# Finished states of a gated graph network turned by VectorE and a DMA trip in place of TensorE transposes

## What is computed

```python
h = relu(layernorm(x))
q, k, v = h @ Wq.T, h @ Wk.T, h @ Wv.T
rel = adj.T * (q @ k.T);  rel = rel / norm(rel, axis=2)
x = x + rel @ v                                   # attention part
h = relu(layernorm(x))
for _ in range(3):                                # gated part
    a  = adj @ h;  av = concat(a, a)
    z  = sigmoid(av @ w3.T + h @ u3.T + biases)
    r  = sigmoid(av @ w4.T + h @ u3.T + biases)
    c  = tanh(av @ w5.T + (r * h) @ u5.T + biases)
    h  = (1 - z) * h + z * c
x = x + h
```

## Time and profile before

| | us |
|---|---|
| median of 3 runs | 982.24 (981.36 to 982.58) |
| the profiled execution | 981.1 |
| its span, first to last instruction | 978.8 |
| TensorE busy | 960.0 (98%) |
| VectorE busy | 678.8 (69%) |
| ScalarE busy | 501.1 (51%) |
| GpSimd busy | 119.8 (12%) |

### The profile page before, as it was taken

The page is one execution under the profiler, slowest core; times in us unless marked ns, Lnnn a source line. Parts: engine busy times, 40 slices in busy tenths (PEclk is TensorE's granted clock), DMA queues, the critical chain, the costliest instruction groups (busy, mean ns, idle before and its releaser), DMA issues.

```text
span 978.8 us, 15089 instructions
## 1 busy us (share of the span) xinstructions
PE 960.0 (98%) x5256; PEld 829.2 (85%) x5256; DVE 678.8 (69%) x1338; ACT 501.1 (51%) x877; POOL 119.8 (12%) x161
## 2 busy tenths in 40 slices
PE   7799999999999999999999999999999999999996
PEld 7788888888888888888888888888888888888885
DVE  4866768776677776877767767776768766676644
ACT  4455554645446463554725645356544555445542
POOL 1210112102030010200102001110111101020000
PEclk9899999999999999999999999999999999999998
DMA  5011111211022020310203102031010311010001
GB/s 168 1 44 44 39 48 41 90 43 64 21 71 87 13 86 0 128 43 0 86 17 111 43 0 86 21 107 43 25 60 21 107 43 57 28 58 28 1 2 43
DMA packets 41537, 49.43 MB, mean 51 GB/s; under 512 B 4400, under 2 KB 37936, under 8 KB 41520
## 3 DMA queue, kind: packets, MB, share of 16 engines
q1 hardware_dynamic: 41520, 49.20, 15.3%
HBM read 26.12 MB, written 23.07 MB: 50 GB/s over the span
## 4 chain that ended last, share of the span: by engine, by line
PE 96%; DVE 1%; ACT 1%; issue 0%; POOL 0%; DVEq 0%; POOLq 0%
PE gate L357 14%; PE gate L359 13%; PE gate L358 13%; PE cand L357 9%; PE cand L359 9%; PE cand L358 9%; PE fea L460 9%; PE tok L453 4%; PE fea L420 3%; PE tok L357 2%; PE tok L358 2%; PE tok L359 2%; PE fea L357 1%; PE fea L358 1%; PE fea L359 1%; PE fea L429 1%
## 5 line engine op out<-in xcount | busy, mean ns | idle before, releaser
L643 ACT ACTIVATE h_hi<-h 128x512 fp32r<-128x512 f32 x92 | 56.6, 633 | 120.3 <-DVE h L1002 92.4
L866 DVE TENSOR_TENSOR d_s<-c_s,h 128x512 f32<-128x512 f32 x96 | 66.4, 705 | 67.3 <-ACT c_s L738 66.9
L719 ACT ACTIVATE r_s<-gate,b_r 128x512 f32<-128x512 f32 x96 | 64.9, 684 | 89.8 <-PE gate L359 89.8
L738 ACT ACTIVATE c_s<-cand,b_c 128x512 f32<-128x512 f32 x96 | 64.8, 684 | 52.9 <-PE cand L359 52.9
L866 DVE TENSOR_TENSOR rh_lo<-rh,rh_hi 128x512 fp32r<-128x512 f32 x96 | 72.3, 792 | 26.4 <-ACT rh_hi L643 25.1
L305 POOL TENSOR_TENSOR rstd<-vare,minus_half 128x4 f32<-128x4 f32 x32 | 33.0, 1032 | 449.7 <-DVE vare L894 449.7
L866 DVE TENSOR_TENSOR a_lo<-fea,a_hi 128x512 fp32r<-128x512 f32 x96 | 64.3, 687 | 34.4 <-ACT a_hi L643 34.4
L357 PE MATMUL gate<-a_hi,W_hi_wz 128*128 128x512 f32 x192 | 79.4, 413 | 0.0
L357 PE MATMUL cand<-rh_hi,W_hi_u 128*128 128x512 f32 x192 | 78.2, 407 | 0.0
L357 PE MATMUL cand<-a_hi,W_hi_w 128*128 128x512 f32 x192 | 78.1, 407 | 0.0
L1008 DVE TENSOR_TENSOR rh<-r_s,h 128x512 f32<-128x512 f32 x96 | 63.6, 681 | 17.6 <-ACT r_s L719 17.6
(11 more groups left out here) (122 smaller groups left out, 2286.6 us busy)
## 6 DMA issues: line engine op xcount, KB each, us to landing
x_s<-x SPq DMA_DIRECT2D x16, 512.0 KB, 5.2
out<-o_s SPq DMA_DIRECT2D x16, 512.0 KB, 3.0
hx_trip<-hx SPq DMA_DIRECT2D x14, 512.0 KB, 2.6
hx_back<-hx_trip SPq DMA_DIRECT2D x56, 128.0 KB, 2.8
h_trip<-h_blk SPq DMA_DIRECT2D x14, 512.0 KB, 2.6
h_back<-h_trip SPq DMA_DIRECT2D x56, 128.0 KB, 2.8
z_s<-w_t SPq DMA_DIRECT2D x1, 512.0 KB, 4.1
r_s<-w_t SPq DMA_DIRECT2D x1, 512.0 KB, 5.0
```

Of the source, the lines that this page charges most:

```text
L643: return nc.scalar.activation(dst, src, ACT.Copy)
L719: nc.scalar.activation(r_s[:, c, :], gate[:, c, :], ACT.Sigmoid, bias=b_r[:, c:c + 1]).then_inc(r_ready, 1)
L738: nc.scalar.activation(c_s[:, c, :], cand[:, c, :], ACT.Tanh, bias=b_c[:, c:c + 1]).then_inc(c_ready, 1)
L866: return nc.vector.tensor_tensor(dst, a, b, ALU.subtract)
```

## The change

- The transposes of `transpose_state` go, except for the last update of the last group. `update` turns each half of the new state with a 32x32 block transpose into `h_turned` right behind the update of that half; SP writes that to DRAM (`h_trip`) and reads it back in four DMAs into `h_back` (`turn_state`), 47 times; ScalarE copies `h_back` to `t_s` in plain order (`take_back`).
- The adjacency product moves to the end of a window, behind `candidate_rh`, in all windows. `split_a` moves with it: on ScalarE behind the tanh, on VectorE behind the next window's update.
- The update becomes z*c - (z-1)*h: `kept_part` computes (z-1)*h ahead, at a window's end; behind the tanh stand a multiplication and a subtraction per half.
- The norm sums go to the PSUM tile `gate` instead of `fea`; TensorE waits for their copy (`norm_taken`) before it starts the next reset gate.
- The residual of all groups but the last is added by GpSimd from `h_back` (`final`), behind which are its copies `keep_resid` and `h0_in_order`.
- On SP the x loads are moved among the trips, and stores wait for GpSimd's `final_ready`.
- `split_state` on VectorE moves behind `split_rh` in windows 1, 2 and 4, statistics and shifts move within their windows.

```diff
         @block.sync
+            def turn_state(w):
+                sp.wait_ge(h_is_turned, 2 * w)
+                sp.dma_start(h_trip, h_turned[:].rearrange("p a q c f -> p (a q c f)")).then_inc(h_out, 16)
+                sp.wait_ge(h_out, 16 * w + 16)
+                blocks_back(h_back, h_trip, h_in)
+            def round_of(i, more=True):
+                turn_state(6 * i + 1)
+                sp.wait_ge(resid_ready, 2 * i + 2)
+                load_x(2 * i + 3, 1)
                 turn_hx(2 * i + 2, 0)
+                turn_state(6 * i + 2)
+                turn_state(6 * i + 3)
                 turn_hx(2 * i + 3, 1)
+                turn_state(6 * i + 4)
                 turn_h0(2 * i + 2, 0)
+                turn_state(6 * i + 5)
                 turn_h0(2 * i + 3, 1)
+                store_final(2 * i, 0)
+                if more:
+                    sp.wait_ge(resid_ready, 2 * i + 3)
+                    load_x(2 * i + 4, 0)
+                turn_state(6 * i + 6)
+                store_final(2 * i + 1, 1)
...
         @block.gpsimd
+            def final(g, s, w, stores):
+                pool.wait_ge(resid_ready, g + 1)
+                pool.wait_ge(stored[s], stores * 16 + 16)
+                pool.wait_ge(h_in, 16 * BL * w)
...
+                for q in range(Q):
+                    last = nc.gpsimd.tensor_tensor(
+                        o_s[s][:, q, :].rearrange("p (c b f) -> p c b f", c=C, b=BL),
+                        h_back[:, :, q, :, :].rearrange("p b c f -> p c b f"),
+                        resid[s][:, q, :].rearrange("p (c b f) -> p c b f", c=C, b=BL), ALU.add)
+                last.then_inc(final_ready, 1)
...
         @block.tensor
             def window(i, k, use, attention=True, new=True):
+                if attention and k == 3:
+                    weighted_sum(2 * i + 2, use("sum X"), use("v X"))
+                    pe.wait_ge(norm_taken, 2 * i + 1)
...
+                reset_gate(w, s, use("adj %d" % (k - 1)) if k > 1 else use_in_round("adj 0" if k else "adj 5", i - 1))
+                update_gate(w, s)
+                candidate_a(w, s)
...
+                candidate_rh(w, s)
...
+                    for c in range(C):
+                        pe.wait_ge(t_ready, 8 * i + 2 * k + (c - 1))
+                        adjacency(c, t_s, use("adj %d" % k))
+                if attention and k == 2:
+                    norms(2 * i + 2, w)
...
         @block.scalar
+            def take_back(w):
+                act.wait_ge(h_in, 16 * BL * w)
+                for c in range(C):
+                    copy(t_s[:, :, c * P:(c + 1) * P].rearrange("p q (b f) -> p q b f", b=BL),
+                         h_back[:, :, :, c, :].rearrange("p b q f -> p q b f")).then_inc(t_ready, 1)
...
         @block.vector
+            def kept_part(w, s):
+                for c in range(C):
+                    dve.wait_ge(z_ready, 2 * w + (c + 1))
+                    nc.vector.scalar_tensor_tensor(d_s[:, c, :], z_s[:, c, :], 1.0, h[s][:, c, :],
+                                                   ALU.subtract, ALU.mult).then_inc(diff_ready, 1)
+            def update(w, o, turned=True):
                 for c in range(C):
                     dve.wait_ge(c_ready, 2 * w + (c - 1))
-                    sub(d_s[:, c, :], c_s[:, c, :], h[o][:, c, :]).then_inc(diff_ready, 1)
...
+                    nc.vector.tensor_tensor(c_s[:, c, :], z_s[:, c, :], c_s[:, c, :], ALU.mult).then_inc(prod_ready, 1)
+                    dve.wait_ge(prod_ready, 2 * w + (c - 1))
                     dve.wait_ge(diff_ready, 2 * w + (c - 1))
...
+                    sub(h[o][:, c, :], c_s[:, c, :], d_s[:, c, :]).then_inc(upd_ready, 1)
+                    if turned:
+                        dve.wait_ge(upd_ready, 2 * w + (c - 1))
+                        if c == 0:
+                            dve.wait_ge(h_out, 16 * w)
+                        nc.vector.transpose(h_turned[:, :, :, c, :].rearrange("p a q f -> p q a f"),
+                                            h[o][:, c, :]).then_inc(h_is_turned, 1)
...
             def window(i, k, use, attention=True, new=True):
                 w, s, o = 6 * i + k, k % 2, 1 - k % 2
+                update(w, o)
+                if attention and k == 3:
+                    take_norm(2 * i + 1)
+                elif attention and k == 5:
+                    take_norm(2 * i + 2)
+                split_a(w, s, 0)
+                split_a(w, s, 1)
```

## The result

The changed kernel takes 995.26 us, median of four runs (993.59 to 998.76), against 982.41 us (four runs, 981.36 to 982.75) for the kernel before on the same chip: a ratio of 1.0137, interval 1.0109 to 1.0166. It is slower, by 12.8 us. The profiled execution took 993.59 us, span 991.6 us, 12.8 us more than the span before. The forecast was 984.9 us in a range of 963 to 1000.

What follows compares the result with a forecast made beforehand. TensorE, busy 98% of the span, was taken to bound the kernel. On 981.1 us, -41.4 - 1.6 + 25.6 + 6.7 + 4.3 + 9.1 = +2.7 gave 983.8; 1.1 for the median made 984.9 us, range 963 to 1000.

Steps and rivals of the forecast that it cites:

- The mechanism: At window boundaries, time taken from TensorE comes back as its waits for VectorE's split or norm copy.
- What is removed: On TensorE, the transposes of 47 windows go, at 0.88 us each: 41.4 us gained.
- A plain boundary: Between windows without attention, TensorE waits 0.80 us for VectorE's a_lo, 32 times: 25.6 us lost.
- Attention boundaries: Where another group's attention lies between windows, TensorE waits 0.48 us for the norm copy, 14 times: 6.7 us.
- The first boundary: After the start code, VectorE's split ends late and TensorE waits 4.3 us, where it had no wait before.
- GpSimd at the group ends: At two group ends a round, GpSimd's copies and adds slow VectorE: 1.3 us per round, 9.1 us in all.
- D: Rival, chance 0.22: GpSimd's adds exceed about 1.3 us, both group-end boundaries hit in full, 3 us per round: 996.8 us.
- C: Rival, chance 0.06: on VectorE a dependent step costs 0.61 us like an independent one, stall 0.2: 958.4 us.
- B: Rival, chance 0.24: same waits at low bounds, plain stall 0.59 us, contention 0.4 a round: 968.8 us.
- F: Rival, chance 0.03: the state's trip takes over 10 us and comes after the tanh is due: 1013 us.
- E: Rival, chance 0.03: stalls at boundaries lower TensorE's clock, 1.5 us at each of 47: 1055 us.
- The tail: After the last candidate, only multiply and subtract stand behind the second tanh: 1.6 us gained.

Runs made afterwards that it cites:

- experiment 1: The changed kernel with both 32x32 transposes of the state moved behind split_a on VectorE: 952.60 us, ratio 0.9698 to the kernel before.
- experiment 6: The changed kernel with transposes behind split_a, residual sums on VectorE, GpSimd's residual copy later and the trip ahead of the load: 939.48 us, ratio 0.9555.
- Experiment 2: The changed kernel with GpSimd's four residual additions per group cut to one over eight columns, output lacking the sums: 977.45 us, ratio 0.9948.
- Experiment 3: The changed kernel with SP issuing the state's trip in window 0 before it waits to load the next x: 992.42 us, ratio 1.0107.
- experiment 7: The changed kernel with the old update (c-h, times z, plus h) and no kept part: 1073.92 us, one execution.
- experiment 5: The changed kernel with both transposes behind split_a and GpSimd's sums cut to eight columns: 937.83 us, ratio 0.9545.

## Why the prediction was right, point by point

**The mechanism: right.** TensorE's saved time came back as waits for VectorE's split at the places named, in the numbers named (33 for a_lo, 14 for the norm), and experiment 1 removes them at the plain and the attention boundaries by the order alone. The sign and the range were right, the size was not: +2.7 was the sum, +12.8 the spans' difference. Part of that is luck. The prediction gave slower 0.47 and faster 0.40, hardly a choice, and a range of 37 us around a sum of +2.7 holds both signs. Its misses also partly cancel: 4.9 us more gained on TensorE and 2.2 less lost in 32 plain stalls stand against 9.6 more beside GpSimd, 6.4 of slow stages and 1.7 more with attention.

**What is removed: somewhat too small.** The rows gave 0.88 a window. From u5's first matmul in one window to that in the next, TensorE's timeline of the kernel before has, for windows without attention:

```profile
935.31 0.39 PE L357 MATMUL cand<-rh_hi,W_hi_u 128*128 128x512 f32 x1
...
951.64 0.39 PE L357 MATMUL cand<-rh_hi,W_hi_u 128*128 128x512 f32 x1
```

These are 16.33 us apart, and in experiment 6 the same windows are 15.40 apart; with 0.02 of lateness taken off, the eight transposes were worth 0.95. Over a whole round of six windows it is 117.71 against 111.8 us, 0.985 a window: 46.3 us in place of 41.4. In the two windows with attention of each round the difference is 1.07. By the starts of the stages in the kernel before, the extra lies mostly at the transposes themselves: between these two rows they take 0.79 us (943.48 to 944.27), and the stage behind them takes 2.85 in place of 2.72; in the second window with attention of a round it is 0.94 (835.55 to 836.49) and 2.87. A rest of under 0.1 a window I did not place. So the prediction's 0.87, and 0.01 for switching, were too small.

**A plain boundary: right.** 0.80 foreseen, 0.73 measured. The steps, from the timeline at 485.06: multiply to subtract 0.73 (0.76 taken), subtract to transpose 0.82, and 0.69 and 0.72 in the second half; the independent ones 0.63, 0.64. a_lo was foreseen at T+5.12 and came at T+5.04.

**Attention boundaries: 0.60 for 0.48,** 1.7 us over the 14. The first state matmul starts 5.29 us after the tanh of the first half (466.48 to 471.77), foreseen 5.30, and TensorE would have been ready 4.83 us after it, foreseen 4.82: the stall is 0.46 for 0.48. The other 0.13 stand behind it, since the twelve state matmuls take 2.85 us in place of 2.72; the sum had no term for that. The rows of that boundary, T = 467.19:

```profile
466.48 0.67 ACT L738 ACTIVATE c_s<-cand,b_c 128x512 f32<-128x512 f32 x1
...
471.41 0.12 DVE L908 COPY norm<-gate 128x4 f32<-128x4 f32 x1
...
471.77 0.49 PE L386 MATMUL gate<-h_hi,W_hi_u 128*128 128x512 f32 x1 [0.30 <-DVE norm L908]
```

**The first boundary: 4.2 for 4.3, and 1.7 that was not in the sum.** VectorE ended the split at 71.76 (71.92 foreseen), TensorE went at 71.81. Without the wait it would have gone at 67.59: the state matmuls start at 64.78, and in the kernel before the a matmuls follow them by 2.81 (64.84 to 67.65; the 67.82 of the earlier trace rows is the end of the matmul before, where the chain begins its piece). Behind it TensorE's timeline shows something new:

```profile
71.81 0.50 PE L386 MATMUL gate<-a_hi,W_hi_w 128*128 128x512 f32 x1 [4.06 <-DVE a_lo L827]
...
72.98 0.63 PE L387 MATMUL gate<-a_lo,W_hi_w 128*128 128x512 f32 x1
73.41 0.63 PE L388 MATMUL gate<-a_hi,W_lo_w 128*128 128x512 f32 x1
...
75.97 0.45 PE L388 MATMUL gate<-a_hi,W_lo_w 128*128 128x512 f32 x1
76.26 0.40 PE L386 MATMUL gate<-a_hi,W_hi_wz 128*128 128x512 f32 x1
```

Matmuls start 0.43 us apart, nearly double the 0.23 of before and after: the granted clock is 0.50 from 72.8 to 76.0, the 1.2 GHz level, after an idle time of 4.06 us.

**GpSimd at the group ends: the term that failed.** Foreseen 1.3 us a round. Measured, over what a plain boundary costs: 1.77-0.73 = 1.04 into window 0 (0.8 foreseen) and, without the slow stages, about 2.36-0.73 = 1.63 into window 1 (0.5 foreseen), so 2.7 a round, 18.7 us for 9.1, and 4.7 us of slow stages behind three of the seven. The step that failed is the placing of the trip in window 0.

Into window 0 the size was nearly right and its make-up was not. The adds push the residual copy onto the kept part, so the update begins 0.30 to 0.32 us after T in all seven, which the prediction had named as a sign of being wrong (later than T-0.4). It had put 0.2 on that late start and 0.6 on slowed operations; at T = 527.35 the late start is 0.75, and the two slowed operations lose 0.27. GpSimd and VectorE there:

```profile
525.08 1.51 POOL L354 COPY resid<-x_s 128x1024 f32<-128x1024 f32 x1
...
527.13 2.81 POOL L329 COPY h<-h_blk 128x256 f32<-128x256 f32 x4
...
525.62 2.12 DVE L960 SCALAR_TENSOR_TENSOR d_s<-z_s,h 128x512 f32<-128x512 f32 x2
527.66 0.88 DVE L967 TENSOR_TENSOR c_s<-z_s,c_s 128x512 f32<-128x512 f32 x1
```

Into window 1, T = 544.47, SP, GpSimd and VectorE of the changed kernel:

```profile
531.05 0.41 SPq L218 DMA_DIRECT2D x_s<-x  x1
532.26 0.34 SPq L243 DMA_DIRECT2D h_trip<-h_turned  x1
538.14 1.75 SPq L226 DMA_DIRECT2D h_back<-h_trip  x4
```

```profile
543.14 3.71 POOL L341 TENSOR_TENSOR o_s<-h_back,resid 128x256 f32<-128x256 f32 x4
...
547.68 1.04 POOL L354 COPY resid<-x_s 128x1024 f32<-128x1024 f32 x1
```

```profile
544.03 1.09 DVE L967 TENSOR_TENSOR c_s<-z_s,c_s 128x512 f32<-128x512 f32 x1 [0.90 <-ACT c_s L738]
545.16 1.11 DVE L827 TENSOR_TENSOR h<-c_s,d_s 128x512 f32<-128x512 f32 x1
546.40 0.71 DVE L975 STREAM_TRANSPOSE h_turned<-h 128x512 f32<-128x512 f32 x1
547.03 0.65 DVE L967 TENSOR_TENSOR c_s<-z_s,c_s 128x512 f32<-128x512 f32 x1
547.72 1.54 DVE L827 TENSOR_TENSOR h<-c_s,d_s 128x512 f32<-128x512 f32 x1
```

The write was priced at 2.7 us. Issued 1.2 us behind the load of x (531.05), it took 5.9 (532.26 to the reads at 538.14; 5.3 to 7.0 in the six rounds with this load), and the adds, foreseen from 13 to 16 us after the boundary at 527.35, ran from 15.8 to 19.5, over the update of the boundary at 17.1. Three of VectorE's operations are slowed, by 0.40 and 0.42 beside the adds and by 0.85 beside the residual copy that follows them: together 1.67 us, which is the 2.26 less 0.60 of this boundary. Experiment 2 shows that the sums are the main cause: 17.8 us of the 23.4 (18.7 and 4.7) go with them, and the other 5.6 stay. Experiment 3 shows that the moment alone is not: an earlier trip changes what they slow.

**The rivals.** D gave 996.8 us and lies nearest to the measured 995.26. Half of its mechanism is there: both boundaries hit in full, at 2.7 a round for its 3. Its condition is not: an add took 0.73 to 1.19 us (3.71 for the four above), below its 1.3, and TensorE never waits for rh_lo in this kernel. So its time lies near partly by chance: 6.4 us of the measured time are slow stages, which it does not have. C is refuted: its stall was 0.2, measured 0.60, and a dependent step took 0.69 to 0.82 in the changed kernel and 0.72 in experiment 7, beside 0.63 for independent ones. (The Trainium skill, "VectorE: DVE Perf Modes", section "The DRAIN you can't avoid", found eight copies equally long with a semaphore after each and with one behind the last. C took from it that a dependent step costs nothing more; for these operations of 512 columns, each reading what the one before wrote, the runs decide against that.) B had the plain lateness, 0.59 for the 0.60 measured, but not the 0.13 behind it, and its 0.4 a round for contention is far below the 2.7. F is refuted: ScalarE's copy of the returned state waits for no DMA, so the trip stays hidden though its write can take 7.0 us. E was far too pessimistic for the 0.6 us stalls, behind none of which the clock fell, and yet a small part of it is real at the long ones, 6.4 us in this kernel (4.7 and 1.7). That is a second term that the sum took at nothing.

**The tail: right.** Its wait is 2.23 us for 3.91, 1.7 us gained for 1.6 foreseen.

## What to carry to other kernels

When work moves from the engine that bounds a kernel to one that feeds it, the price is not the moved work but its place in the feeder's list. An operation without an urgent reader, placed ahead of one with such a reader, costs at every repetition what it exceeds of the slack there: at a plain boundary the two transposes put a_lo 1.5 us later, TensorE had nearly 1.0 in hand, and 0.6 of wait was left (42.7 us in all). The engine's busy share says nothing of it. Look for each new operation at who reads it and when, and put what is read late behind what is read soon. In this kernel, work on GpSimd beside a VectorE that is on the critical path was paid for by VectorE. It was cheaper to give VectorE the adds themselves (30 of them at 0.68, 20 us, in slack) than to have GpSimd do them beside it (14.8 us of the span, from experiments 1 and 5). Experiment 6 also moves the copy and the trip, so how much of its gain each of these has is not shown.

## What the runs showed of the hardware

A two-input add of 128x256 on GpSimd took 0.73 us with VectorE idle or at a transpose, and up to 1.19 beside VectorE's two-input operations. Those took 0.8 to 1.25 us beside the adds in place of 0.69, and up to 1.54 beside the residual copy. VectorE's 32x32 transposes were not slowed: sixteen that lay wholly beside GpSimd's adds took 0.67 to 0.71. The same sums on VectorE took 0.68 us for 128x512; GpSimd took 1.5 to 2.4 for as many elements.

After a wait of TensorE for VectorE the stage of 12 matmuls behind it took 0.12 to 0.17 us more than one without a wait, also where the wait was 0.6 us. In the changed kernel the granted clock fell to half only behind the longest: at the first boundary (4.06 us idle) and behind three of the seven into window 1. There the lateness was 2.25 to 2.56 us, but others with 2.26 kept the full clock. The length of the wait does not decide alone: in experiment 7 seven stages behind an idle time of only 1.87 us fell to half clock in window 2, each one window behind an idle time of 2.2 to 5.5 us, and of the eleven others behind 1.87 only one did. What tells them apart stays open. Runs differ in the clock as well as in time: 993.59 at a mean clock of 0.986, 998.76 at 0.980.

A write of 512 KB to DRAM landed in a median of 2.7 us, and in 5.3 to 7.0 us in the six cases where a load of the same size was issued 0.5 to 1.2 us before it; issued ahead of that load, in experiment 3, it took 2.8 to 3.5.
